# Four graph layers on one core: neighbour rounds in another order, own scores in two parts, and a last attention block without units or records

## The reference

```python
h = relu(layernorm(x)); x = x + L0(h)   # attention over both directions of every edge, 4 heads, then two dense layers with a Gelu
h = relu(layernorm(x)); x = x + L1(h)   # two rounds: h = relu([h, mean over edges of h[src], mean of edge attributes] @ W + b)
h = relu(layernorm(x)); x = x + L2(h)   # one round: mean over edges of ([h, h[src] - h] @ W + b), 0 without edges
h = relu(layernorm(x)); x = x + L3(h)   # attention over incoming edges and a loop, 8 heads; e = leaky(a_src[src] + a_dst[dst]),
                                        # softmax by dst, weighted sum of h[src], dense layers, two layer norms
```

## Time and profile before

| | |
|---|---|
| three runs | 5446.4, 5452.0, 5456.73 us; median 5452.0 |
| profiled execution, its own time | 5456.45 us |
| its span, first to last instruction | 5454.2 us |
| mean granted clock of TensorE | 0.62 |
| busy: VectorE, POOL, TensorE, ScalarE | 74%, 65%, 46%, 23% |

### The profile page before, as it was taken

The page is one execution under the profiler, slowest core; times in us unless marked ns, Lnnn a source line. Parts: engine busy times, 40 slices in busy tenths (PEclk is TensorE's granted clock), DMA queues, the critical chain, the costliest instruction groups (busy, mean ns, idle before and its releaser), DMA issues.

```text
span 5454.2 us, 51431 instructions
## 1 busy us (share of the span) xinstructions
PE 2509.3 (46%) x13080; PEld 1714.4 (31%) x13080; DVE 4020.0 (74%) x7076; ACT 1273.8 (23%) x4458; POOL 3568.5 (65%) x3780
## 2 busy tenths in 40 slices
PE   1697110101212133433333335449982777777765
PEld 0572000101212132322223234437771333333324
DVE  9877888887887587878778787835552677777776
ACT  0000000000000011111111111110001878777761
POOL 2777777777777777777777777430005777777743
PEclk6555555555555555555555555559995888888885
DMA  7212121121222232232322333227771222222222
GB/s 252 58 54 58 47 56 49 48 72 42 54 62 58 59 83 74 82 82 80 84 74 80 83 81 84 89 61 247 258 236 23 79 87 88 87 80 88 87 72 60
DMA packets 392241, 476.93 MB, mean 87 GB/s; under 512 B 216403, under 2 KB 252309, under 8 KB 384838
## 3 DMA queue, kind: packets, MB, share of 16 engines
q1 hardware_dynamic: 136422, 279.67, 15.2%
q0 software_dynamic: 114832, 133.36, 10.8%
q10 hardware_dynamic: 140752, 61.28, 4.0%
HBM read 294.77 MB, written 179.24 MB: 87 GB/s over the span
## 4 chain that ended last, share of the span: by engine, by line
POOL 51%; issue 20%; DVE 15%; PE 10%; DMA 3%; ACT 0%; POOLq 0%; DVEq 0%; ACTq 0%; SPq 0%
POOL arena L807 35%; POOL rec_dram L764 13%; PE acc L2288 4%; DVE OHX L1564 3%; PE pw L2276 2%; DVE oh L1574 1%; DVE arena L1586 1%; DVE V L1606 1%; DVE arena L1590 1%; POOL own_dram L784 1%; DVE sc L1591 1%; DMA arena<-tab_dram,jst 1%; DVE oh L1564 1%; PE acc L2230 1%; PE acc L2095 1%
## 5 line engine op out<-in xcount | busy, mean ns | idle before, releaser
L807 POOL DMA_INDIRECT arena<-tab_dram,jst x2592 | 2470.6, 953 | 778.3 <-issue 772.8
L764 POOL DMA_INDIRECT rec_dram<-V,rowst x784 | 837.7, 1068 | 231.9 <-issue 226.1
L2222 PE MATMUL pw<-OHX 128*128 128x128 bf16 x1632 | 209.0, 308 | 790.9 <-DVE OHX L1564 790.2
L2230 PE MATMUL acc<-arena,oh 128*128 128x64 f32 x1952 | 426.7, 420 | 252.5 <-DVE oh L1574 252.5
L2230 PEld LDWEIGHTS acc<-arena,oh 128*128 128x128 f32 x1952 | 416.8, 329 | 266.8 <-issue 266.8
L999 ACT ACTIVATE arena<-arena,ew 128x64 f32<-128x64 f32 x1728 | 417.8, 334 | 38.3 <-PE acc L2322 38.3
L2222 PEld LDWEIGHTS pw<-OHX 128*128 128x128 bf16 x1632 | 155.7, 140 | 841.8 <-DVE OHX L1564 841.8
L999 ACT ACTIVATE OHX<-arena,ew 128x64 f32<-128x64 f32 x1728 | 417.8, 333 | 2.5
L1586 DVE TENSOR_TENSOR arena<-arena,pt 128x1024 f32<-128x1024 f32 x108 | 131.8, 1221 | 380.4 <-DMA arena<-tab_dram,jst 378.3
L2322 PE MATMUL acc<-OHX,ident 128*128 128x512 f32 x432 | 259.5, 768 | 310.8 <-ACT OHX L999 262.7
L2322 PE MATMUL acc<-arena,ident 128*128 128x512 f32 x864 | 382.1, 595 | 29.6 <-ACT arena L999 23.1
(11 more groups left out here) (588 smaller groups left out, 5951.7 us busy)
## 6 DMA issues: line engine op xcount, KB each, us to landing
arena<-tab_dram,jst POOLq DMA_INDIRECT x2592
arena<-rec_dram SPq DMA_DIRECT2D x122, 288.0 KB, 3.8
mt_dram<-oh ACTq DMA_DIRECT2D x272, 128.0 KB, 1.7
rows_dram<-V SPq DMA_DIRECT2D x27, 1056.0 KB, 4.1
rows_dram<-arena SPq DMA_DIRECT2D x27, 1056.0 KB
V<-in_edge_attr_dram ACTq DMA_DIRECT2D x97, 256.0 KB
oh<-mt_dram SPq DMA_DIRECT2D x42, 512.0 KB, 4.7
OHX<-mt_dram SPq DMA_DIRECT2D x38, 512.0 KB, 4.7
```

The costliest lines, as they stand in the source:

```text
L764: gp.indirect_dma_start(rec[:, :], bass.IndirectOffsetOnAxis(ap=rowst[:, q, k:k + 1], axis=0), recst[:, q, k, :], None).then_inc(S[f"scat{ ...
L807: gp.indirect_dma_start(hd.G[:, a.r, j, :], None, table[:, :], row_of(jst[:, a.r, j:j + 1])).then_inc(S[f"rows{a.r}"], 16)
L2222: last = nc.tensor.matmul(unit_bank(c.slot)[:, k // 2 * P:(k // 2 + 1) * P], mones[c.slot][:, 0, k, :], mones[c.slot][:, 1, k, :], start=k ...
L2230: last = nc.tensor.matmul(o, roh[:, c.q, k, :], RG[:, c.r, k, 0:D], start=False, stop=True, skip_group_check=True)
```

## The change

- **Last block.** `LAST` is 44 and `ULR` gives 4, 4, 4, 3, 4, 4, 4, 3, 4, 0 records to blocks 44 to 53; `unit_at` ends the units in block 52. SP's loop is unrolled from block 40 on.
- **Between attention and rounds.** Transposes, Gelu (pieces of 512 and 384 columns), product, norm and split are done for the front 16 chunks and then the rear 9. The maximum with zero and the scaling are one instruction (`rescaled`).
- **Order of the rounds.** Four half-cells (the first halves of chunks 0 to 3, `LEAD`) come first and need the front's split only; then pairs of over-blocks behind one half-cell, four times, and behind two, ten times, and a single one at the end. There are 29 over-blocks instead of 30. A pair reads its 32 source chunks in one load. Two chunks share a PSUM bank while the leading ones are summed.
- **End of a round.** The over-sums of the front are reduced in two parts with a taking between; the rear's are reduced before the front's layer; the transposes come after half-cell 37, the front's product after 39. Features live in the left half of `CAT` (`HC`); the copy at the start of a round is gone.
- **Own scores.** ACT copies them from PSUM and fills the table, for the front (`asd` 1 to 3) and the rear (4 to 6). POOL scatters 16 chunks when the front is there and 9 when the rear is. On TensorE the front's transposes and scores stand before the rear's dense product. SP loads the first three lists before all that.

```diff
-OVB = 30
+OVB = 29
-ITEMS = [x for t in range(OVB) for x in (("cell", t), ("over", t))] + [("cell", t) for t in range(OVB, NBS)]
-ADVANCE, FORM = 35, 37
+LEAD = 4
+CORDER = [2 * c for c in range(LEAD)] + [2 * c + 1 for c in range(LEAD)] + list(range(2 * LEAD, NBS))
+OVERS = [range(t, min(t + 2, OVB)) for t in range(0, OVB, 2)]
+def turn_order():
+    left, shift = iter(CORDER), LEAD
+    yield from (("cell", next(left)) for _ in range(LEAD))
+    for pair in OVERS:
+        yield "cell", next(left)
+        if shift == 0 and len(pair) == 2:
+            yield "cell", next(left)
+        shift = max(shift - 1, 0)
+        yield from (("over", t) for t in pair)
+    yield from (("cell", t) for t in left)
+ADVANCE, FORM = 37, 39
-ULR = (0, 4, 9, 13, 18, 22, 26)
-LAST = NB0 - 6
+ULR = (0, 4, 8, 12, 15, 19, 23, 27, 30, 34, 34)
+LAST = NB0 - 10
-            return max(g - UNITS_AT, 0) * NU // (NB0 - UNITS_AT)
+            return min(max(g - UNITS_AT, 0) * NU // (NB0 - 1 - UNITS_AT), NU)
...
-            table(8, TB3, tab[1])
-            table(8, AS[:, :, H3:2 * H3], tabd)
+            for b in range(3):
+                load_meta(heads3, Group(0, b))
+            for k, cs in enumerate(PARTS):
+                sp.wait_ge(S["asd"], 3 * k + 1)
+                sp.dma_start(tabd[nodes]..., AS[:, cs, H3:2 * H3]).then_inc(S["tb"], 16)
+                sp.wait_ge(S["asd"], 3 * k + 3)
+                sp.dma_start(tab[1][nodes]..., TB3[:, cs]).then_inc(S["tb"], 16)
             sp.wait_ge(S["dosc"], 16 * NC)
...
-            held_for(S["tsrc"], 8)
-            for c in range(NC):
-                gp.indirect_dma_start(own3[:, :], row_of(rst_u[:, 2, c:c + 1]), AS[:, c, H3:2 * H3], None).then_inc(S["dosc"], 16)
-            held_for(S["tb"], 5 * 16)
+            for k, cs in enumerate(PARTS):
+                held_for(S["asd"], 3 * k + 1)
+                for c in range(NC)[cs]:
+                    gp.indirect_dma_start(own3[:, :], row_of(rst_u[:, 2, c:c + 1]), AS[:, c, H3:2 * H3], None).then_inc(S["dosc"], 16)
+            held_for(S["tb"], 7 * 16)
...
+            def own_scores(k, cs):
+                act.wait_ge(S["lin"], 12 + 2 * k)
+                A.copy(AS[:, cs], got).then_inc(S["asd"], 1)
+                A.copy(TB3[:, cs, D:D + H3], got[:, :, 0:H3]).then_inc(S["asd"], 1)
+                A.copy(TB3[:, cs, 0:D], Hn[:, cs, :]).then_inc(S["asd"], 1)
...
-            norm(Hn[:], X[:])
-            split_high(0, slice(0, NC))
-            split_low(0, slice(0, NC))
+            def rescaled(dst, cs):
+                v.wait_ge(S["lns"], nln[0])
+                link(V.reciprocal(st[:, 3, cs], st[:, 2, cs]))
+                link(V.scalar_tensor_tensor(dst, XC[:, cs], 0.0, over(st[:, 3], cs), ALU.max, ALU.mult))
+            for k, cs in enumerate(PARTS):
+                v.wait_ge(S["lin"], 5 + k)
+                link(V.tensor_tensor(X[:, cs, :], X[:, cs, :], acc_n[:, cs], ALU.add))
+                centred(X[:, cs, :], cs)
+                variance(cs)
+                rescaled(HC[:, cs, :], cs)
+                split_high(0, cs)
+                split_low(0, cs)
...
-                link(V.tensor_copy(CAT[:, :, 0:D], Hn[:]))
...
+                v.wait_ge(S["oadd"], (r + 1) * OVG)
+                for cs in (slice(0, 8), slice(8, front.stop)):
+                    over_sums(cs)
+                    take_chunk(next(late))
+                means(front, front.stop, lambda: take_chunk(next(late)))
+                take_chunk(next(late))
+                over_sums(rear)
...
-            v.wait_ge(S["lin"], 13)
-            link(V.tensor_copy(AS[:], acc[:, 0:NC * 2 * H3].rearrange("p (c h) -> p c h", h=2 * H3)))
-            link(V.tensor_copy(TB3[:, :, 0:D], Hn[:]))
-            V.tensor_copy(TB3[:, :, D:D + H3], AS[:, :, 0:H3]).then_inc(S["tsrc"], 1)
+            v.wait_ge(S["asd"], 6)
...
-                    rows = nc.values_load_multi_w_load_instructions(
-                        jtab[0:1, at_ * BT:(at_ + 1) * BT], engines=[mybir.EngineType.PE], ...
+                    if at_ % 2 == 0:
+                        rows[:] = nc.values_load_multi_w_load_instructions(
+                            jtab[0:1, at_ * BT:min(at_ + 2, OVB) * BT], engines=[mybir.EngineType.PE], ...
...
-                pe.wait_ge(S["ev"], 6 + 2 * r)
+                if r == 2:
+                    pe.wait_ge(S["ev"], 10)
+                    transposes(Hn[:], D, part=batches[0])
+                pe.wait_ge(S["ev"], 6 + 2 * r + (r == 2))
                 transposes(CAT, 2 * D, part=batches[1])
+                if r == 2:
+                    product([(T, D, Asd[:].rearrange("p s h -> p (s h)"))], 2 * H3, range(NC)[PARTS[0]])
                 product([(T, 2 * D, layer_w)], D, range(NC)[PARTS[1]])
```

More of the change, by code:

```diff
@@ L309, in build @@
         ZF = arena[:, 12800:13312]
+        HC = CAT[:, :, 0:D]
         wraw = OHXf[0:D, 0:7 * D]
@@ L410, in quads, with spans @@
                     body(Group(n // 4, t))
-        def spans(eng, n, ahead, step, cut=4, between=None):
+        def spans(eng, n, ahead, step, cut=4, between=None, loops=None):
             def at(i, t):
                 step(lambda d: Group(i, t + d) if not (isinstance(i, int) and 4 * i + t + d >= n) else None)
-            whole = (n - ahead) // 4
+            whole = loops or (n - ahead) // 4
             for t in range(4):
@@ L1806, in _ @@
                     if what == "over":
                         add_group(at_)
-                    elif at_ % 2:
+                    elif at_ in (3, 7):
+                        take_chunk(at_ // 2 - 1)
                         take_chunk(at_ // 2)
-                for c in range(OVB // 2, front.stop):
-                    take_chunk(c)
-                v.wait_ge(S["oadd"], (r + 1) * OVG)
-                over_sums(front)
-                v.wait_ge(S["osr"], 2 * r + 1)
-                means(front, front.stop)
@@ L1816, in _ @@
-                for c in range(front.stop, (FORM + 1) // 2):
-                    take_chunk(c)
-                over_sums(rear)
+                    elif at_ % 2 and at_ > 7:
+                        take_chunk(at_ // 2)
+                late = iter(range(OVB // 2, NC))
+                v.wait_ge(S["oadd"], (r + 1) * OVG)
[3 more added lines that the diff above has]
+                means(front, front.stop, lambda: take_chunk(next(late)))
@@ L1819, in _ @@
+                take_chunk(next(late))
+                over_sums(rear)
+                for c in (18, 19):
+                    assert next(late) == c
+                    take_chunk(c)
                 layer(front, 1)
-                late = iter(range((FORM + 1) // 2, NC))
                 take_chunk(next(late))
@@ L1826, in _ @@
                 else:
-                    onto_x(front)
-                    take_chunk(next(late))
                     centred(X[:, front, :], front)
@@ L2087, in transposes, with product @@
                     ntp[0] += 1
-            def product(parts, width, chunks=range(NC)):
+            def product(parts, width, chunks=range(NC), at_=0):
                 pe.wait_ge(S["tc"], ntp[0])
                 for c in chunks:
-                    o = acc[:, c * width:(c + 1) * width]
+                    o = acc[:, at_ + c * width:at_ + (c + 1) * width]
                     for n, (TL, K, R) in enumerate(parts):
```

181 lines of the change are left out of this document (91 added, 90 removed).

## The result

The changed kernel took 5378.9 us (median of 4 runs, 5374.36 to 5382.66) where the kernel before took 5449.2 beside it (4 runs): ratio 0.9866 as recorded, 95% interval 0.9854 to 0.9879 (the two medians divide to 0.9871, inside it). That is 70 us less, where 99 were forecast: inside the range of 5328 to 5386, 26 us above the forecast of 5353. The profiled executions (span 5454.2 before, 5380.6 after) differ by 73.6 us, and the traces give it stage by stage.

A forecast was written before the change was run, and what follows sets the result against it. POOL's gather issue was taken to bound both attentions, so gains lie around them and in the rounds: 23.6 + 17.4 + 6.6 + 12.6 + 14 + 24.8 = 99.0 us off the profiled 5456.45, forecast 5353 at run level, range 5328 to 5386.

The forecast's parts named there:

- 1, last block: End of first attention: last block without units and records, lag gone (6.6 us) and weighting earlier (17.0); 23.6 us together.
- 2, between attention and rounds: First attention's output to round 1: front half processed while rear gathers run; 17.4 us, or 13.8 without the leading half-cells' gain.
- 3.6 us for leading half-cells: Before round 1's over-blocks: three more half-cells already done, at 1.2 us each, added to the 13.8 of earlier start.
- 3, in the rounds: Three rounds: one over-block less each (6.6 us) and joint loads at 0.3 a pair (12.6, bounds 0 to 39).
- 0.93 taken as the upper bound: Over-block loads in the rounds: joining two was to save at most 0.93 us a load; 0.3 was taken.
- rival (c): Own scores: scatter's parts don't overlap, sixteen scatters (20.2 us) still stand behind the rear; about 5373 us, chance 0.06.
- signs of being wrong: Granted clock 0.5 in rounds, a transfer wait before a cell, or a gap between sixteenth and seventeenth scatter would refute it.
- (e): Rounds: slower, TensorE misses the high clock level because its new order leaves waits; 5551 us for three rounds, chance 0.03.
- (a): Rounds don't run faster inside: a load of 32 costs two of 16, or transfers hold pace; about 5366 us, chance 0.16.
- (b): Rounds: the load was dearer; at 0.6 a pair about 5340 us, at 0.93 5327; chance 0.10.
- 4, ends of rounds: Ends of rounds 1 and 2, starts of 2 and 3: less idle time, more half-cells done; 14 us (bounds 7 and 17).
- 5, own scores: Rear means to second attention's first gather: sixteen scatters beside the rear layer, 68.6 to 45.8 us; 24.8 with round 3's end.

## Why the prediction came out as it did

**1, last block: right.** 22.7 for 23.6. VectorE began block 53 42.1 us behind that block's first gather instead of 47.7: 5.6 of the 6.6 of lag went, the four-record blocks taking 40.3 and the three-record ones 36.8. The exponentials were followed at once by the weighting, as worked out. Undoing it cost 22 us.

**2, between attention and rounds: right up to the first over-block** (13.5 for 13.8). VectorE's small tensor-scalar did stand beside POOL's zeroing: it took 1.77 us for the 0.17 it takes elsewhere and ended at 3612.48, the zeroing at 3612.45; the one in round 1 of the kernel before had ended 0.54 us behind its zeroing. The wait for the square root covered part of the longer time, 0.62 being left. The 3.6 us for leading half-cells are the part that failed, below.

**3, in the rounds: wrong, and the whole miss.** The step that failed reads "The load's cost is not shown; the 0.32 is what sticks out of it". It took the part of a load that sticks out for what joining two loads saves, gave the pairing no term, and the half-cells that leave the phase were priced (in steps 2 and 4) at their full 1.2 us each. The cost stood in the trace of before, 1.10 us at TensorE's sequencer, above even the 0.93 taken as the upper bound. What sticks out of a load is not what it costs, since the half-cell ahead hid 0.88 of it. The runs split the row of the table, summed over the three rounds:

| Part | runs compared | gain | forecast |
|---|---|---|---|
| one over-block and five half-cells less | before, and 16 a load with a half-cell before each | 12.8 | 19.8 |
| joint load | 16 and 32 a load, in either order | 4.3 | 12.6 |
| pairing | a half-cell before each, and pair order, with either load | -14.0 | 0 |
| sum | | 3.1 | 32.4 |

The pairing costs because the second half-cell of a pair hides only some 0.5 us more (1.35 idle behind one, 0.89 behind two) while the second over-block lost its cover. The half-cells gave little because inside the phase they are nearly free: in the run with one before every over-block, four more in each round cost 0.5 to 0.9 us, each covering a load that stood bare. The sum also miscounted them: it moves three out of the phase in round 1 and four in the others, but five left it in each, since one more stands before the first pair and, in round 1, the one that moved behind the phase was left out. Taken apart by rows, as an estimate, the over-block is worth 3.1 a round (1.10 of load and 2.0 of issue; 2.2 forecast), which leaves 1.2 for five half-cells.

That the time lies within the range is luck. The upper bound of 5386 was made of the load's saving gone and rival (c), and (c) didn't happen; the pairing's loss stood in no bound. The prediction's signs of being wrong (a granted clock of 0.5 inside the rounds, a wait for a transfer, a gap between scatters) didn't show, but for the 7 us named below under (e), and the sign of being right, no 0.32 before the second over-block of a pair, came true while the time was lost before the first.

Of the rivals, (a) named the right half, that a load of 32 costs two of 16; its price was "no gain" where the pairing made a loss of it. Its other half, the transfers, was refuted: they ran at some 250 to 280 GB/s with TensorE waiting for issue, and reached 349 in the run without loads. (b) had the price nearer, the load being dearer than even its 0.93, and the wrong sign: a dear load that is joined is still paid by the number (1.10 for 16, 2.13 for 32). (e) hardly happened: the granted clock was 0.98 to 1.00 over the over-phases. Only in round 3, behind 3.36 us of waiting between the leading half-cells and the first pair, was it 0.61 for 7 us (3923 to 3930), and the first pair's matmuls took 5.30 us where round 1's took 4.37.

**4, ends of rounds: right between the rounds, a little better** (6.3 for 4.4). The other 9.6 of its 14 were the half-cells, which failed with step 3. The 4.4 are 1.2 into round 2 and 3.2 into round 3, worked out from idle times of 3.70 and 9.82 us before the first over-blocks, at a mean granted clock of 0.50 (the prediction's low level; its high level is 1.00). No run shows the terms behind them one by one; the two stretches got 2.5 and 3.8 us shorter, and TensorE's weight loads stood idle for 0.89 us before the first over-block of round 2, and for 3.58 and 1.44 around the last leading half-cell of round 3. In round 1 the front transposes stood without the 2.54 of idle, and the relu took 0.69 us instead of 2.29, away from POOL's zeroing.

**5, own scores: right, 28.0 for 24.8.** The front scores took 5.89 us of TensorE at a mean granted clock of 0.60, where the row taken for them was 7.00 at 0.50, and 16 + 9 scatters ran without a gap. The rear scores were there at 4081.3, before POOL asked at 4085.0: "with little to spare", as worked out.

**What the sum left out.** The 2.1 us up to block 53 and 2.2 in the rear gathers (POOL had single gathers of 2.50 and 1.99 us for 0.94) were lost, and 4.2 behind the second attention's first gather gained. The last of these is partly the clock: the final product of 32 matmuls took 3.76 us at a granted clock of 1.00 in the profiled run of the changed kernel and 7.06 at 0.50 in that of before. Unlike what the section on the time before says, the rounds are not the only place at the full clock: before, the mean granted clock was 0.94 in the rounds and 0.83 in the second attention. The three cancel but for 0.1 and aren't put down to the change.

## What to carry to other kernels

Before pricing a change to loads or register addresses, ask the trace for the sequencer's own rows (by tile of the table that is loaded, by line of the matmuls): what an engine idles behind an instruction is only the part that sticks out (here 0.32 us of a load of 1.10), and work that looks removable may be the cover of something else. Joining two loads saved only 0.076 us a pair here. What helped was fewer numbers (0.064 us each), a shorter address computation (9 ns a matmul), and matmuls ahead of each load (a half-cell hid 0.88 us of it). When the bound of a phase is issue, as in these over-phases, work that costs little issue can ride along almost free (here 0.2 us for a half-cell that takes 1.0), above all where it covers a load; taking it out gains little.

## What the runs showed of the hardware that was not expected

- Loading numbers from a table into TensorE's registers took 0.591, 1.104 and 2.132 us for 8, 16 and 32 (the run with loads of 8, the kernel before, the changed kernel): by these three, 0.064 us a number and under 0.08 fixed.
- The address of a matmul, computed from a register, took 46 ns of the sequencer (before and changed kernel), and 37 ns with one multiplication less; an over-block's matmul with such an address came every 0.125 and 0.117 us (16 weight loads in 2.00 and 1.87), one without every 0.083 (20 in 1.67, the run without loads).
- A second half-cell ahead of a load of 2.13 us hid only about 0.5 us more of it (0.89 of idle time instead of 1.35, changed kernel, round 1), though it lasts 1.0. Behind one half-cell the load started at the sequencer with the half-cell's weight loads (3637.6 and 3637.55), 1.0 us ahead of their end; behind two it started 0.6 us later than theirs (3672.3 and 3671.70), 1.4 ahead of their end.
- After 3.43 us of idle time inside a round, 25 weight loads took 3.39 us instead of 2.08, in a stretch of 10 us at a mean granted clock of 0.83 (the run with a half-cell before every over-block, round 1).
